# A three-hop graph network on one core: weights between the steps of norms, the scaling put off from the last softmax, the last norms in two parts, and the additions of out by tile

## What is computed

```python
rel = edge_emb[edge_type]
agg = entity_emb                      # relu(layernorm(x))
out = 0
for _ in range(3):
    left = agg[head] @ q_w
    right = tanh(rel * agg[tail] @ k_w)
    att = sum(left * right, axis=1)
    w = softmax of att over the edges of one head
    summed = segment_sum(w[:, None] * rel * agg[tail], head)
    agg = summed / max(cnt, 1)
    agg = agg / max(norm(agg), 1e-12)
    out = out + agg + entity_emb
return x + out
```

## Time and profile before

| | us |
|---|---|
| median of 3 runs | 2604.02 |
| lowest and highest | 2588.33, 2604.54 |
| the profiled execution | 2568.1 |
| its span, first to last instruction | 2566.3 |

### The profile page before, as it was taken

How to read it: one execution, slowest core, us unless ns; L and a number is a source line. 1 busy time by engine, 2 the same in 40 slices (tenths; PEclk the granted TensorE clock), 3 DMA queues, 4 the chain that set the end, 5 groups by cost and what they waited for, 6 DMA issues and landing times. The chain is left out here.

```text
span 2566.3 us, 24723 instructions
## 1 busy us (share of the span) xinstructions
PE 1126.9 (44%) x5196; PEld 897.6 (35%) x5196; DVE 1454.0 (57%) x7228; ACT 858.7 (33%) x2657; POOL 1190.2 (46%) x1219
## 2 busy tenths in 40 slices
PE   0112333355454545553100257688734667655430
PEld 0011222244344324453100135467623455454320
DVE  8863664453364545544339657667654644657664
ACT  3312442332333423333126433344433232222320
POOL 1034434454545354466650255552035554647666
PEclk9999655555565655556555577788567777765555
DMA  5532322221222222322225464453144644636654
GB/s 203 207 139 88 129 93 67 68 80 57 71 67 68 71 71 70 115 80 92 77 81 213 172 189 146 132 150 109 63 153 139 189 127 115 174 85 168 168 142 130
DMA packets 192463, 305.35 MB, mean 119 GB/s; under 512 B 31210, under 2 KB 113458, under 8 KB 183686
## 3 DMA queue, kind: packets, MB, share of 16 engines
q1 hardware_dynamic: 153914, 230.79, 26.9%
q0 software_dynamic: 38400, 72.99, 10.8%
HBM read 176.41 MB, written 132.67 MB: 120 GB/s over the span
## 5 line engine op out<-in xcount | busy, mean ns | idle before, releaser
L646 POOL DMA_INDIRECT tr<-in_x_dram,tidx x200 | 191.4, 957 | 508.4 <-DMA acc_d<-xr 297.1
L1574 PE MATMUL ps<-rt,wr 128*125 128x128 f32 x1200 | 266.3, 392 | 245.1 <-issue 85.0
L1503 PE MATMUL ps<-ident,rt 128*128 128x128 f32 x600 | 144.6, 385 | 449.2 <-DVE rt L1169 206.8
L646 POOL DMA_INDIRECT tr<-agg_d,tidx x200 | 191.9, 959 | 288.4 <-DMA agg_d<-rt 138.4
L1574 PEld LDWEIGHTS ps<-rt,wr 128*125 128x125 f32 x1200 | 233.0, 288 | 263.4 <-DVE wr L1094 145.5
L1381 ACT ACTIVATE sqj<-ps,invc 125x128 bf16<-125x128 f32 x600 | 212.3, 373 | 328.5 <-remote 161.1
L646 POOL DMA_INDIRECT tr<-ntab_d,tidx x200 | 193.7, 969 | 260.9 <-DVE rt L1169 196.3
L1341 ACT COPY turns<-ps 128x512 f32<-128x512 f32 x150 | 87.8, 585 | 617.1 <-PE ps L1503 351.1
L1503 PEld LDWEIGHTS ps<-ident,rt 128*128 128x128 f32 x600 | 98.0, 196 | 482.0 <-issue 248.4
L1094 DVE TENSOR_SCALAR wr<-segbc,lcol,wcol 128x125 f32<-128x125 uint8 x600 | 177.9, 349 | 153.7 <-remote 111.4
L658 POOL DMA_INDIRECT ntab_d<-rt,lidx x200 | 202.1, 1011 | 134.2 <-DVE rt L1118 75.1
(11 more groups left out here) (239 smaller groups left out, 2456.2 us busy)
## 6 DMA issues: line engine op xcount, KB each, us to landing
agg_d<-rt SPq DMA_DIRECT2D x100, 258.0 KB
xr<-agg_d SPq DMA_DIRECT2D x100, 258.0 KB
relr<-rel_d SPq DMA_DIRECT2D x100, 256.0 KB
ntab_d<-rt SPq DMA_DIRECT2D x10, 2519.5 KB
acc_d<-xr SPq DMA_DIRECT2D x50, 258.0 KB
rel_d<-relr SPq DMA_DIRECT2D x50, 256.0 KB
hr<-acc_d SPq DMA_DIRECT2D x50, 256.0 KB
hr<-agg_d SPq DMA_DIRECT2D x50, 256.0 KB
```

Of the source, the lines that this page charges most:

```text
L646: G.indirect_dma_start(out=row, out_offset=None, in_=table[:, :], in_offset=bass.IndirectOffsetOnAxis(ap=idx[:, n:n + 1], axis=0)).then_in ...
L1503: ins = T.transpose(ps[B_TR][:, t, :], rt[:, g * GT + t, 0:D], ident[:, :])
L1574: ins = T.matmul(ps[B_T + j % 2][0:R, t, :], wr[:, (j % 2) * GT + t, 0:R], rt[:, j * GT + t, 0:D], start=True, stop=True)
```

## The change

Four edits, all on VectorE's list. The lists of the other engines stay as they are.

1. norms takes the groups it is for, and a list of work to put between its steps: each step issues, then one piece of the other work, then waits for the step. sums(h, j) hands it weights(h, j), so where sums has norms to do, the weights of group j are issued inside the chain, behind the wait for s_nr. Where there are no norms, weights come first as before.
2. In the last softmax only the weights are issued behind a stage. The scaling of the five groups is put off to the mixed groups, two to each until none is left; in hop 1 one remains and comes before carries.
3. The last norms of a hop, of groups 45 to 49, are made in two parts: for 45 to 47, which are scaled at once, and for 48 and 49.
4. In hop 2, one_in and two_in are added by tile: four additions of 125 x 128 each with a wait between the two sets, in place of one of 125 x 512 each.

```diff
-            def norms(h, i):
+            def norms(h, some, between=()):
+
+                between = list(between)
+
+                def step(ins):
+                    ch.note(ins)
+                    done = ch.at
+                    if between:
+                        between.pop(0)()
+                    dve.wait_ge(s_dve, done)
+                dve.wait_ge(s_nr, h * NG + some[-1] + 1)
+                u = some[0] // NB
+                here = slice((some[0] - u * NB) * GT, (some[-1] + 1 - u * NB) * GT)
...
                 ch.join()
-                ch(V.tensor_tensor(edge_rows(j)[0:R], edge_rows(j)[0:R], one_in[j % 2][0:R], ALU.add))
-                V.tensor_tensor(edge_rows(j)[0:R], edge_rows(j)[0:R], two_in[j % 2][0:R], ALU.add).then_inc(s_ag, 1)
-
-            def scaled(h, j):
+                for t in range(GT):
+                    n = j * GT + t
+                    ch.note(V.tensor_tensor(rt[0:R, n, 0:D], rt[0:R, n, 0:D], one_in[j % 2][0:R, t, :], ALU.add))
+                ch.join()
+                for t in range(GT):
+                    n = j * GT + t
+                    ins = V.tensor_tensor(rt[0:R, n, 0:D], rt[0:R, n, 0:D], two_in[j % 2][0:R, t, :], ALU.add)
+                ins.then_inc(s_ag, 1)
+
+            def scaled(h, j, between=()):
+                if j >= LAG and (j - LAG) % NB == 0:
+                    norms(h, range(j - LAG, j - LAG + NB), between)
+                else:
+                    for work in between:
+                        work()
                 if j >= LAG:
-                    if (j - LAG) % NB == 0:
-                        norms(h, (j - LAG) // NB)
                     scale(h, j - LAG)
 
             def sums(h, j):
-                for work in weights(h, j):
-                    work()
-                scaled(h, j)
+                scaled(h, j, weights(h, j))
...
                 for i in range(STAGES):
                     softmax(h, LAST, i)
                     for j in sum_behind(h, i):
-                        sums(h, j)
+                        for work in weights(h, j):
+                            work()
+                put_off = list(sums_left(h)[:FILL])
                 for j in sums_mixed(h):
-                    sums(h, j)
+                    for work in weights(h, j):
+                        work()
+                    put_off.append(j)
+                    for k in put_off[:2]:
+                        scaled(h, k)
+                    put_off = put_off[2:]
+                for k in put_off:
+                    scaled(h, k)
                 carries(h, LAST)
                 for j in (*sums_held(h), *range(GC[LAST], NG)):
                     sums(h, j)
                 scale(h, NG - LAG)
-                norms(h, NG // NB - 1)
-                for j in range(NG - NB, NG):
-                    scale(h, j)
+                for some in (range(NG - NB, NG - 2), range(NG - 2, NG)):
+                    norms(h, some)
+                    for j in some:
+                        scale(h, j)
```

16 lines of the change are left out of this document (8 added, 8 removed).

## The result

The changed kernel took 2639.64 us (median of 4 runs, 2633.02 to 2661.03), the kernel before 2598.43 us (4 runs, 2588.33 to 2604.54). The medians lie 41 us apart; the ratio of the executions is 1.0193, 95% interval 1.0135 to 1.025, which is 50 us (35 to 65). So the change makes the kernel some 40 to 50 us slower, where 6 us (2610.0) had been forecast; the result lies 1.6 us above the range, and next to the time that the slower rival gave (2633).

What follows compares the result with a forecast made beforehand. The end was taken as VectorE's scaling of group 40 in hop 2 plus POOL's last 40 scatters. Hop 0 -5.3, hop 1 -3.6 and hop 2 +15.0 gave +6.1: 2574.2, scaled 2610.0 us, range 2572 to 2638.

Steps and rivals of the forecast that it cites:

- the slower rival: Added VectorE instructions arrive late, costing 14.0 us, and a 10.7 us wait falls ahead of group 40: 2633 us; chance 0.24.
- Putting off, hop 1 (-4.6): Last softmax of hop 1: stages shorten by 4.6 us; the put-off scaling is covered by TensorE's work behind.
- Putting off, hop 2 (+3.8): Hop 2: idle VectorE time +2.7, load waits +2.7, fewer TensorE waits -1.6; POOL's late group 8 does not count.
- Putting off, hop 0 (-4.6): Last softmax of hop 0: stages shorten by 4.6 us; later scaling covered, POOL waits for VectorE at later groups anyway.
- Additions by tile (+10.5): Hop 2: 0.37 us more per group over 33 groups, +12.2 us, less 1.7 us absorbed by load waits.
- Load waits (+2.7 within the +3.8, and -1.7 within the +10.5): Hop 2, VectorE: back-to-back scalings wait 0.9 us in three pairs; longer scaling absorbs 1.7 us of waits before group 40.
- Instructions (+2.7, bounds 0 and 14.0): Hop 2: 198 added VectorE instructions ahead of group 40 might lengthen unexplained waits by 5.4 us; half taken.
- Shorter scatters (-2.0): Hop 2, POOL's last 40 scatters: shorter additions hold them up less, gaining 2 us; bounds 0 and 3.4.
- Norms (-0.2, -1.1, +1.2): Last norms in two parts: -0.2 us hop 1, -1.1 hop 0; weights behind ACT's squares: +1.2 in each.
- What would show it: Profile after: hop 1 softmax stages 4.6 us shorter, scaling 2.8 us, scatters near 1.0 us, POOL waiting at groups 26 and 40.
- three signs of being wrong: Additions not 0.20 us apart; POOL never waiting in hop 2 after group 8; hop 0's long waits growing or going.
- The likeliest case: The forecast itself, in which VectorE's time up to group 40 decides: 2595 to 2625 us, chance 0.42.

Runs made afterwards that it cites:

- e8_put2: Scaling put off from the last softmax in hop 2 only, on the kernel before (2595.69 us on that chip): ratio 1.0015, +4 us.
- e2_put_off: Scaling put off from the last softmax in all three hops, nothing else, on the kernel before (1968.66 us on that chip): ratio 1.0042, +8 us.
- e4_hold: Kernel before (1968.66 us there), with only POOL held ahead of group 8 in hop 2 until VectorE has scaled group 12: ratio 1.009, +17.7 us.
- f2_adds: Only the additions of hop 2 made by tile, on the kernel before (2605.96 us on that chip): ratio 1.0099, +26 us.
- e9_put0: Scaling put off from the last softmax in hop 0 only, on the kernel before (2595.69 us on that chip): ratio 1.0039, +10 us.
- f6_time: Kernel before (2585.69 us there) plus one 256-element VectorE instruction ahead of each hop 2 group's first addition, about as long as the split additions add: ratio 0.9984.
- the six fills: Kernel before (1968.85 and 1966.97 us there) plus six one-column VectorE fills ahead of the first addition of each hop 2 group: ratios 0.9989 and 1.003.
- e1_adds: Only the additions of hop 2 made by tile, on the kernel before (1968.66 us on that chip): ratio 0.9995.
- f5_after: The whole change against the kernel before (1966.97 us on that chip): ratio 1.004, +8 us.
- e6_after_put1: The whole change, but with scaling put off in hop 1 alone, against the kernel before (2595.69 us on that chip): ratio 1.0091, +24 us.
- e3_norms: Only the norms changed (weights between their steps, last norms in two parts), on the kernel before (1968.66 us on that chip): ratio 1.0001.

## Why the prediction missed, point by point

**Putting off, hop 1 (-4.6): right.** The walk through the stages held. The last softmax, from the start of the first stage to the start of the copy to wcol, took 20.5 us before and 16.1 us in after; by the prediction's own measure, from the end of the weights ahead of the first stage to stage 6, it is 12.7 us where 13.3 had been forecast, and 17.9 before. Its timeline has the forecast releaser, TensorE. The wait of 0.39 us is new, the one of 1.58 us was 0.87 before, and the one ahead of wcol (0.48 us) was there before:

```profile
1847.40 1.11 DVE L1094 TENSOR_SCALAR wr<-segbc,lcol,wcol 128x125 f32<-128x125 uint8 x4 [0.15 <-DVE rcar L972]
1848.90 0.15 DVE L979 TENSOR_TENSOR seg_xf<-seg_x,ps 44x1 f32<-44x1 f32 x1 [0.39 <-PE ps L1519]
...
1856.62 0.15 DVE L979 TENSOR_TENSOR seg_xf<-seg_x,ps 44x1 f32<-44x1 f32 x1 [1.58 <-PE ps L1519]
...
1860.05 0.20 DVE L988 COPY wcol<-ps 128x44 f32<-128x44 f32 x1 [0.48 <-PE ps L1525]
```

**Putting off, hop 2 (+3.8): this step failed.** The prediction saw that POOL would get group 8 some 18 us later and dismissed it with one sentence: it "stands still for VectorE again later, 8.51 us at group 40, so VectorE's time still decides". On waiting chips the sentence is right for the whole change, since POOL still starts group 40 as soon as VectorE has scaled it. What was wrong there is VectorE's own lateness: 11.0 us at group 40 in e8_put2 where the sum had +3.8, and POOL's queue adds 3. By the traces the right term was +14. By the total on a waiting chip (+4, -7 to +15) the forecast +3.8 can't be excluded. On quiet chips the sentence is wrong: POOL's later stops aren't there, VectorE is only 8.7 us later at group 40 in e2_put_off and has 31 us to spare, and e4_hold shows the pure case, 17.7 us later (10 to 25) for a stop that is 23.0 us longer.

**Putting off, hop 0 (-4.6): this step failed on waiting chips.** The stages got shorter as forecast, but POOL stood still 15.2 us ahead of group 8, and the prediction had "waits for VectorE at later groups anyway" for it. On a waiting chip hop 0's scatters took 16.5 us longer and the total +10 (-1 to +21). The length of hop 0's scatters splits by this part alone: 336.3 to 345.3 us in the five waiting traces without it, 349.2 to 356.9 in the four with it. On quiet chips VectorE's dense tiles and the rest of hop 1's start covered it, as the prediction would have it (287.2 us against 268.3, then 411.6 against 431.9 in e2_put_off).

**Additions by tile (+10.5): the time of one was nearly right, the total not; with the instructions below it is the largest error by the measured totals.** One scaling now takes 2.94 us from L1136 to the next weights (2.8 forecast), with 0.93 and 0.84 us for the two additions (0.91 and 0.80 forecast), so 0.44 us more per group instead of 0.37. VectorE's timeline in hop 2:

```profile
2447.11 1.14 DVE L1136 SCALAR_TENSOR_TENSOR rt<-rt,nsc,hr 125x128 f32<-125x128 f32 x4
2448.28 0.90 DVE L1141 TENSOR_TENSOR rt<-rt,hr 125x128 f32<-125x128 f32 x4
2449.21 0.91 DVE L1145 TENSOR_TENSOR rt<-rt,ohT 125x128 f32<-125x128 f32 x4
2450.05 1.10 DVE L1094 TENSOR_SCALAR wr<-segbc,lcol,wcol 128x125 f32<-128x125 uint8 x4
```

In the trace of f2_adds VectorE has scaled group 40 9.1 us later than in before, near the forecast, and hop 2 is 13 us longer. The rest stands where the prediction expected nothing: it said that "what VectorE does after group 40 in hop 2 is covered by that queue", and in all five traces with the additions by tile POOL waits again behind group 40 and is 3 to 6 us longer from there to its last scatter (4.4 us of waiting ahead of group 43 in f2_adds). On quiet chips no cost shows in the total: POOL is the bound there and VectorE's time lies under it.

**Load waits (+2.7 within the +3.8, and -1.7 within the +10.5): the first came, the second did not.** Over the whole window VectorE waited 9.6 us for the transfers to ohT in nine places, the longest 2.6, against 8.9 us in eight. But between POOL's first scatter and VectorE's end of group 40 it is 5.8, 4.7 and 5.9 us in the three traces of the whole change, against 1.2 in before and 3.6 in e9_put0, whose hop 2 is the same as before's. The line for the whole window, in after:

```profile
DVE rt L1136 <- DMA ohT<-agg_d: 9.6, 9, 2.6
```

**Instructions (+2.7, bounds 0 and 14.0): mis-sized, and perhaps put in the wrong place.** The additions alone cost 26 us (15 to 37) on a waiting chip, and their time alone costs nothing there (f6_time, -15 to +6). In the trace of f2_adds 13 us of hop 2 and 13 us ahead of the first scatter stand against before, the latter in code that the edit doesn't touch. I had looked for this cost only where the instructions stand. Whether it is the number of instructions or something else in the split additions, no run tells: f2_adds and f6_time differ in both, and no row shows a late arrival of instructions, which was the slower rival's mechanism. The bounds also left out one wait of VectorE without a releaser in the same list (3.8 us, cT L1076). The Trainium skill ("Runtime: NRT & Kernel Launch", Instruction fetch mechanics) describes fetching as mostly hidden; the six fills on quiet chips agree (ratios 0.9989 and 1.003, no difference), and for waiting chips no kernel with fills alone was measured.

**Shorter scatters (-2.0): there, and larger where POOL is the bound.** The mean fell from 1043 to 1040, 1032 and 1037 ns in the three traces of the whole change on waiting chips, and from 1058 to 1025 ns on a quiet one. Scatters of over 1.3 us fell from 16 to 7 in after. The forecast said none but beside weights: five of the seven start just after weights have begun and last 2.0 to 2.9 us, the other two (1.4 and 1.5 us) just after a scaling instruction. The Trainium skill ("SBUF — State Buffer", Who interferes with whom) infers that a tensor_tensor with both inputs in SBUF does not hold up descriptor generation, by which the mean would not change; the 33 ns of e1_adds speak against it, 6.6 us over 200 scatters.

**Norms (-0.2, -1.1, +1.2): neutral**, 1.0001 on a quiet chip. On a waiting chip they were not run alone.

**What would show it:** POOL waiting ahead of group 40 came true (8.3 us), ahead of group 26 it did not (0.3 us). Of the three signs of being wrong, "if POOL never waited again in hop 2 after group 8" is what quiet chips show once the scaling is put off (e2_put_off, f5_after). "If the long waits of hop 0 grew" can't be called either way. VectorE's longest was 18.9 us and is 22.06 us in after, but all its waits without a releaser between the first scatter and the first gather of hop 1 add up to 159.8 us in before and to 147.2, 157.7 and 171.1 in the three traces of the whole change:

```profile
1128.91 1.11 DVE L1094 TENSOR_SCALAR wr<-segbc,lcol,wcol 128x125 f32<-128x125 uint8 x4 [22.06 <-remote]
```

**The sum.** The parts measured on waiting chips, additions +26, putting off in hop 0 +10 and in hop 2 +4, with hop 1's -4.4 from the traces, make +35; the whole change measured +50, +33 and +30 by its ratios. The parts have intervals of some 11 us to either side, the whole of 15 to 17, so this closes no better than that. e6_after_put1 agrees: on one chip all but the putting off in hops 0 and 2 costs +24 of the +33. Against the forecast's terms, the additions with their instructions and shorter scatters lacked 15 us (26 instead of 11.2), hop 0's putting off lacked 15 us (+10 instead of -4.6), and hop 2's lacks nothing by the total (+4) and 10 us by the trace (+14). The traces of the whole change put it more sharply. Hop 2 took 321.6 and 321.4 us in the two with before's hop 2, and 358.0, 358.0 and 352.9 in the three of the whole change, so the +15.0 forecast for hop 2 was +31 to +36, more than the +27 that its two parts make in their own traces. What the two cost together beyond that isn't explained. The likeliest case had no room for POOL's late start. The slower rival came within 7 us of the result, but its mechanism is not shown, so its price is luck as far as is known.

## What to carry to other kernels

Before an edit lets a producer finish its groups later, look at who consumes them and count its remaining work. Then ask at one late group which of the two is ahead: when the producer has finished it, and when the consumer starts it. On quiet chips the producer was 31 us ahead at group 40, and a stop of the consumer that was 23.0 us longer cost 17.7 us (e4_hold). On waiting chips the consumer started as soon as the producer had finished, so the producer's own lateness was the cost, and moving its work made it 11 us late where 4 had been forecast. Count also what becomes slower behind the mark that you compare at. Put work off where nobody is fed by it (hop 1 here, where POOL scatters nothing), and test such a claim by holding the consumer alone. Look in a trace of a control experiment whether it does what it was built for: the six fills were to cost 0.35 us a group and cost 0.01.

When a trace is full of waits without a releaser, measure on another chip as well: here 8 of some 30 to 50 us are left where those waits don't exist.

## What the runs showed of the hardware that was not expected

The same program takes 1966.97 to 1968.85 us on three chips and 2585.69 to 2605.96 us on the others, at a mean granted clock of 0.69 and 0.65. What sets the chips apart isn't shown. On quiet chips VectorE's list of waits has no line without a releaser among its longest (e3_norms):

```profile
DVE hidx L1213 <- PE ps L1537: 82.3, 38, 8.5
DVE fxr L1083 <- PE ps L1578: 46.5, 12, 7.5
DVE rt L1182 <- ACT tr L1348: 37.5, 27, 4.4
```

On waiting chips these waits fall where POOL goes on issuing its indirect DMAs. In before, POOL's stops of over 2 us make up 35% of the time from 300 us on, but hold only 51 of the 411 us of VectorE's long waits. In one place the instructions themselves come slowly. Just ahead of the 22.06 us wait, VectorE starts eight scaling instructions that wait for nobody 1.4 us apart, where the distance is 0.2 us otherwise; three of them (after, hop 0):

```profile
1099.31 0.31 DVE L1130 TENSOR_SCALAR rt<-rt,nsc 125x128 f32<-125x128 f32 x1 [1.12 <-issue]
1100.76 0.29 DVE L1130 TENSOR_SCALAR rt<-rt,nsc 125x128 f32<-125x128 f32 x1 [1.14 <-issue]
1102.16 0.29 DVE L1130 TENSOR_SCALAR rt<-rt,nsc 125x128 f32<-125x128 f32 x1 [1.12 <-issue]
```

The wait ends at 1128.91, for ScalarE at 1128.90, and POOL's last scatter ahead of its next stop had ended at 1123.56, 5.3 us earlier. Four of before's waits in hop 0 end likewise 1.3 to 3.9 us after the end of the last scatter ahead of a stop of POOL (at 1111.28, 1142.40, 1173.54 and 1251.28); others, the longest among them (at 1230.28), end while POOL goes on. In the 22 us from 1108 to 1130 the queues carried these packets, and none of instructions (DMA queues of after in that window: packets, MB, share):

```profile
q0 software_dynamic: 416, 0.65, 9.2%
q1 hardware_dynamic: 288, 0.53, 6.5%
```

So no transfer of instructions that the trace records ended this wait. What it is, and why the additions by tile cost more on these chips than their time, stays open: the six fills, which would tell the number of instructions from all else in the additions, met a quiet chip both times, and hop 2 of f6_time is 12 us longer in its trace without a longer total.
